# A sliding-window attention block in a fused fp32 kernel: rotary parts summed by transposes in PSUM, and the keys' cosine product on GpSimd

## What is computed

```python
def attn_layer(x, Wqkv, qs, ksc, Wo):
    q, k, v = jnp.split(x @ Wqkv, 3, -1)        # 16 heads of 64
    q, k, v = (sh(q), sh(k), sh(v))
    q = l2norm(q) * qs
    k = l2norm(k) * ksc
    freqs, scale = rotary_tables(n)
    cos, sin = (jnp.cos(freqs), jnp.sin(freqs))
    q = q * cos * scale + rotate_half(q) * sin * scale
    inv = 1.0 / scale
    k = k * cos * inv + rotate_half(k) * sin * inv
    out = local_attention(q, k, v)              # windows of 32: each sees itself and the one before
    return out.transpose(0, 2, 1, 3).reshape(b, n, INNER) @ Wo
```

## Time and profile before

| | us |
|---|---|
| median of 3 runs | 5173.48 |
| lowest and highest | 5169.82, 5185.4 |
| the profiled execution | 5172.85 |
| its span, first to last instruction | 5170.8 |

### The profile page before, as it was taken

One profiled execution on the slowest core, in us unless ns is written; L12 is line 12 of the kernel. 1 busy time (PEld: TensorE's weight loads), 2 busy tenths in 40 slices (PEclk: granted clock), 3 DMA queues, 4 the chain that ended last, 5 costly groups with the idle time before them and its releaser, 6 DMA issues. The chain is left out here.

```text
span 5170.8 us, 110439 instructions
## 1 busy us (share of the span) xinstructions
PE 3934.8 (76%) x39280; PEld 2903.7 (56%) x39280; DVE 4374.4 (85%) x7725; ACT 3040.4 (59%) x4888; POOL 2537.9 (49%) x1612
## 2 busy tenths in 40 slices
PE   5777777777777777767858678777787787777787
PEld 4655655656656646625535466466465565565565
DVE  8988989979979979954335399799799899898897
ACT  4765756746747747722413477477476476575575
POOL 5645646636636636611010266366366365464562
PEclk8988999989989989986978899899899998899899
DMA  1000000000000000021030000000000000000000
GB/s 47 8 23 11 7 22 12 8 27 6 7 27 7 8 25 8 8 62 26 2 74 1 33 7 7 26 8 21 13 8 20 14 8 19 15 7 22 12 7 12
DMA packets 30608, 88.57 MB, mean 17 GB/s; under 512 B 7505, under 2 KB 13649, under 8 KB 28369
## 3 DMA queue, kind: packets, MB, share of 16 engines
q1 hardware_dynamic: 29104, 80.95, 5.9%
q10 hardware_dynamic: 1152, 3.15, 0.2%
HBM read 38.72 MB, written 1.05 MB: 8 GB/s over the span
## 5 line engine op out<-in xcount | busy, mean ns | idle before, releaser
L771 POOL TENSOR_TENSOR pool<-pool 128x512 f32<-128x512 f32 x768 | 1069.1, 1413 | 968.3 <-DVE pool L869 968.3
L776 POOL TENSOR_TENSOR pool<-pool 128x1024 f32<-128x1024 f32 x384 | 1072.8, 2794 | 168.0 <-DVE pool L880 147.2
L443 PE MATMUL psum<-squares,pool 128*128 128x128 f32 x3072 | 475.4, 304 | 420.8 <-POOL pool L776 259.9
L443 PEld LDWEIGHTS psum<-squares,pool 128*128 128x128 f32 x3072 | 368.9, 153 | 587.2 <-issue 338.1
L880 DVE TENSOR_TENSOR pool<-pool 128x1024 f32<-128x1024 f32 x384 | 678.6, 1806 | 6.8
L483 PE MATMUL psum<-wqkv_hi,xs_lo 128*128 128x512 f32 x1152 | 522.2, 453 | 200.3 <-DVE pool L849 104.6
L646 ACT COPY pool<-psum 64x512 f32<-64x512 f32 x768 | 447.1, 582 | 367.1 <-PE psum L443 361.7
L474 PE MATMUL psum<-pool 128*64 128x128 f32 x6144 | 560.7, 296 | 116.7 <-ACT pool L661 116.5
L420 PE MATMUL psum<-pool 128*128 128x128 f32 x3072 | 455.4, 309 | 130.2 <-ACT pool L646 129.8
L859 DVE TENSOR_REDUCE pool<-pool 128x16 f32<-128x1024 f32 x384 | 449.9, 1210 | 88.1 <-ACT pool L685 88.0
L420 PEld LDWEIGHTS psum<-pool 128*128 128x128 f32 x3072 | 420.4, 219 | 179.4 <-ACT pool L646 167.8
(11 more groups left out here) (165 smaller groups left out, 8247.6 us busy)
## 6 DMA issues: line engine op xcount, KB each, us to landing
pool<-pool SPq DMA_DIRECT2D x192, 128.0 KB, 2.3
pool<-in_wqkv SPq DMA_DIRECT2D x12, 1536.0 KB, 6.0
k_st<-turn_st SPq DMA_DIRECT2D x8, 1536.0 KB, 21.3
pool<-in_wo SPq DMA_DIRECT2D x12, 512.0 KB, 3.6
pool<-in_w SPq DMA_DIRECT2D x12, 341.0 KB, 3.0
pool<-in_w SPq DMA_DIRECT2D x12, 192.0 KB, 2.9
rotary<-in_rotary SPq DMA_DIRECT2D x2, 1024.0 KB, 5.4
pool<-in_scale SPq DMA_DIRECT2D x12, 128.0 KB, 6.2
```

What stands on the lines that cost most here:

```text
L443: last = pe.transpose(bank(7 - p % 2)[:, P * j:P * j + P], rot[:, p // 2, 2 * c:2 * c + 2, :], ident)
L771: last = g.tensor_tensor(rot[:, q, :, hd * r:hd * r + hd], qn[:, q, :, hd * (1 - r):hd * (2 - r)], tab, ALU.mult)
L776: g.tensor_tensor(rot[:, q], rot[:, q], by_cos[:, q], ALU.add).then_inc(rot_ready, 1)
```

## The change

Three things, in the local layers alone.
1. The tensor `rot` becomes `by_sin`: the sine products stay apart from the cosine products, and the add on GpSimd is gone, with `rot_ready`.
2. Each square of 128x128 is written by two transposing matmuls with the identity: one of `by_cos` that starts the accumulation and one of `by_sin` that adds onto it in PSUM. So 32 instructions stand where 16 did, and TensorE waits for the sine products and the cosine products instead of the sum.
3. The keys' cosine product moves from VectorE to GpSimd, behind its four sine products, with a semaphore of its own (`k_cos_ready`). `cos_ready` is now raised once per unit. VectorE's one cosine product waits for the second group of query transposes of the unit before, where it waited for the keys' sum. The waits of the tables, of SyncE's load and of `qn` on `cos_ready` are split into two.

```diff
@@ tables
-                eng.wait_ge(cos_ready, done(layer * UNITS - 1, 2, 1))
+                eng.wait_ge(cos_ready, done(layer * UNITS - 1))
+                eng.wait_ge(k_cos_ready, done(layer * UNITS - 1))
@@ sync, before load_projections
                         sp.wait_ge(sin_ready, done(last, 2, 1))
-                        sp.wait_ge(cos_ready, done(last, 2, 1))
+                        plain(sp)
+                        sp.wait_ge(cos_ready, done(last))
+                        sp.wait_ge(k_cos_ready, done(last))
@@ tensor, turned_scores
-                            pe.wait_ge(rot_ready, done(U, 2, 0))
+                            pe.wait_ge(sin_ready, done(U, 2, 0))
+                            pe.wait_ge(cos_ready, done(U))
...
-                                    pe.wait_ge(rot_ready, done(U, 2, 1))
+                                    pe.wait_ge(sin_ready, done(U, 2, 1))
+                                    pe.wait_ge(k_cos_ready, done(U))
...
-                                    last = pe.transpose(bank(7 - p % 2)[:, P * j:P * j + P],
-                                                        rot[:, p // 2, 2 * c:2 * c + 2, :], ident)
+                                    o = bank(7 - p % 2)[:, P * j:P * j + P]
+                                    pe.matmul(o, by_cos[:, p // 2, 2 * c:2 * c + 2, :], ident,
+                                              start=True, stop=False, is_transpose=True)
+                                    last = pe.matmul(o, by_sin[:, p // 2, 2 * c:2 * c + 2, :], ident,
+                                                     start=False, stop=True, is_transpose=True)
@@ gpsimd, step
-                                        last = g.tensor_tensor(rot[:, q, :, hd * r:hd * r + hd],
+                                        last = g.tensor_tensor(by_sin[:, q, :, hd * r:hd * r + hd],
                                                                qn[:, q, :, hd * (1 - r):hd * (2 - r)], tab, ALU.mult)
                                     last.then_inc(sin_ready, 1)
-                                    g.wait_ge(sin_ready, done(U, 2, q))
-                                    g.wait_ge(cos_ready, done(U, 2, q))
-                                    g.tensor_tensor(rot[:, q], rot[:, q], by_cos[:, q], ALU.add).then_inc(rot_ready, 1)
+                                tab = turn[:, bass.ds(t, 1), 1, :].broadcast_to([P, HEADS, DH])
+                                g.tensor_tensor(by_cos[:, 1], qn[:, 1], tab, ALU.mult).then_inc(k_cos_ready, 1)
@@ vector, step
                                 v.wait_ge(sin_ready, done(U - 1, 2, 1))
-                                v.wait_ge(cos_ready, done(U - 1, 2, 1))
+                                v.wait_ge(k_cos_ready, done(U - 1))
+                                v.wait_ge(cos_ready, done(U - 1))
...
-                                v.wait_ge(rot_ready, done(U - 1, 2, 1))
-                                for q in range(2):
-                                    tab = turn[:, bass.ds(t, 1), q, :].broadcast_to([P, HEADS, DH])
-                                    v.tensor_tensor(by_cos[:, q], qn[:, q], tab, ALU.mult).then_inc(cos_ready, 1)
+                                v.wait_ge(t_ready, done(U - 1, 4, 1))
+                                tab = turn[:, bass.ds(t, 1), 0, :].broadcast_to([P, HEADS, DH])
+                                v.tensor_tensor(by_cos[:, 0], qn[:, 0], tab, ALU.mult).then_inc(cos_ready, 1)
```

More of the change, by code:

```diff
@@ L61, in macaron_program @@
         sq_ready, qn_ready, cos_ready = sem("sq_ready"), sem("qn_ready"), sem("cos_ready")
-        sin_ready, rot_ready, turn_ready = sem("sin_ready"), sem("rot_ready"), sem("turn_ready")
+        k_cos_ready = sem("k_cos_ready")
+        sin_ready, turn_ready = sem("sin_ready"), sem("turn_ready")
         t_ready, t_out, v_out = sem("t_ready"), sem("t_out"), sem("v_out")
@@ L98, in macaron_program @@
                        xc_ready, diag_ready, xn_ready, hid_ready, x_ready, var_step, aff_step],
-            "gpsimd": [lo_ready, w_hi, w_split, sin_ready, rot_ready, turn_ready, k_kept],
+            "gpsimd": [lo_ready, w_hi, w_split, sin_ready, k_cos_ready, turn_ready, k_kept],
         }
@@ L270, in window_half @@
             by_cos = cut(2, HEADS, DH)
-            rot = cut(2, HEADS, DH)
+            by_sin = cut(2, HEADS, DH)
             ss = cut(2 * HEADS)
```

## The result

The changed kernel takes 4698.61 us (median of 4 runs, 4692.60 to 4706.53), where the kernel before takes 5177.23 (median of 4, 5169.82 to 5185.40). The ratio is 0.9076, with a 95% interval of 0.9055 to 0.9097. The forecast was 4731. The profiled execution has a span of 4693.8 us.

What follows compares the result with a forecast made beforehand. VectorE was taken to bound the kernel at 18.27 us per unit. Per layer, first step 2.4, fourteen steps 29.4 and end 5 make 36.8; twelve layers save 442 of 5172.85, giving 4731 us, range 4630 to 4890.

Steps and rivals of the forecast that it cites:

- L146's wait of 1.59: VectorE's tiny instruction (L145 before the change) waits 1.59 us per unit for GpSimd's add; forecast to go with that add.
- The ring of 16.1 us: Chain of ScalarE and TensorE work from unit to unit, hidden by VectorE before; forecast to set the unit at 16.1 us.
- eight parts: Ring's terms: probability copies 5.18, squares 1.94, exponents 1.35, values' copy 0.62, query transposes 1.78, V products 0.79, key transposes 1.13, copies 3.28.
- the third rival: On TensorE, transposes that add cost 0.225 us each, the ring grows to 18.9 and the time is 5250; chance 0.05.
- GpSimd's product 2.4: The keys' cosine product, moved to GpSimd, takes 2.4 us there, bounds 2.38 and 2.58.
- The new wait of 1.5 us at L144's successor: VectorE, reaching L144 at 922.7, waits 1.5 us per unit for GpSimd's keys' cosine product, which ends at 924.2.
- VectorE's round 15.8: VectorE's own time per unit after the change: 18.27 - 2.37 - 1.59 + 1.5 = 15.8 us, below the ring.
- the race: VectorE's cosine product went ahead of GpSimd's second sine product by a hair at 916.78; falling behind costs 1.2 us more.
- The first rival: VectorE stays the bound: its cosine product falls behind GpSimd's second sine product, round 17.0 us, time 4883; chance 0.15.
- The second rival: TensorE's clock keeps dropping to half speed in one unit of three, 17.2 us per unit, time 4916; chance 0.08.
- The ends: Layer ends, where GpSimd's three long weight instructions catch VectorE: forecast gain 5 us per layer, bounds 1 and 9.
- The first steps: Each layer's first step, with nothing behind it, loses VectorE's second cosine product (L880): 2.4 us.

## Why the prediction was right

- **VectorE bounds the kernel before, partly by waiting for GpSimd.** Right. L146's wait of 1.59 is gone. The run with the keys' product moved alone shows the same waits growing when GpSimd gets more.
- **The ring of 16.1 us is next and sets the unit.** Right, with each of its eight parts within 0.06 us; 16.01 in sum. ScalarE waits for transposes alone, 12 transposes more in the ring add 1.33 (8 add 0.89), and 0.6 us more on VectorE add nothing in the middle of a layer.
- **A transpose that adds costs 0.11.** Right; the third rival (0.225 each) falls by the rows.
- **GpSimd's product 2.4.** Measured 2.39.
- **The new wait of 1.5 us at L144's successor, VectorE's round 15.8.** The place was wrong, and the size a third too large. L145 doesn't wait. The wait, 1.03 us, is at the cosine product, which lost the race for which the forecast gave it a hair's lead: L888 takes over 2 us in 135 of 192 units (mean 2003 ns). The round is about 15.4 in the changed kernel (16.01 less 0.6 idle), 15.6 where nothing idles. The error didn't reach the time, because either round is shorter than the ring.
- **The first rival (VectorE stays the bound at 17.0).** Its mechanism, the lost race, came about, its price didn't. It put 1.2 us on top of a round that already held the 1.5 of the other wait. But the two are alternatives: VectorE pays for the same overlap with GpSimd once, at L888 or at L145. The run with two copies less, in which VectorE doesn't idle, shows it pay either way at the same mean, 15.6. In the run with `residual` moved it pays at neither, as its 1.2 us of idle time leave GpSimd the room.
- **The clock doesn't drop.** Right: the slices of the local layers stand at 9 on the page (the lower ones lie in the global attention and at its end), the four units above have 1.00, and the span has 0.953 against 0.913. The second rival falls, and the run with the transposes doubled shows that they alone are enough for it.
- **The sum.** 442 us forecast, 477 measured between the spans. Three terms were off. All fourteen steps were taken at 16.1, but the second and third of a layer take 14.6 and 15.4, before the pipeline is full: 2.2 us a layer, 26 of the 31 by which the steps gave more (384 for 353). The ends gave 69 rather than 60 (6.1 each, but only 2 before the global attention). The first steps gave 2.0 rather than 2.4, 4 less in all.

At the ends, GpSimd's three long instructions for the next layer's weights hold up VectorE less. GpSimd and VectorE of the changed kernel, then VectorE of the kernel before:

```profile
958.95 3.37 DVE L904 TENSOR_SCALAR pool<-squares,pool 128x128 f32<-128x128 f32 x4
959.45 2.78 POOL L305 CAST wqkv_hi<-pool 128x3072 fp32r<-128x3072 f32 x1 [7.49 <-DMA pool<-in_scale]
...
962.41 5.62 POOL L310 TENSOR_TENSOR wqkv_lo<-pool,wqkv_hi 128x3072 fp32r<-128x3072 f32 x1 [0.18 <-POOL wqkv_hi L305]
...
965.96 2.36 DVE L911 TENSOR_SCALAR pool<-pool 128x512 f32<-128x512 f32 x1
968.00 4.71 POOL L317 TENSOR_TENSOR pool<-rotary,pool 128x2048 f32<-128x2048 f32 x1
969.83 4.16 DVE L823 TENSOR_TENSOR pool<-pool 128x256 f32<-128x256 f32 x4
```

```profile
1077.88 2.75 DVE L154 SCALAR_TENSOR_TENSOR pool<-pool 128x4 f32<-128x4 f32 x1
...
1080.87 5.58 DVE L153 TENSOR_TENSOR pool<-pool 128x4 f32<-128x4 f32 x1
```

With the 4.43 of the earlier trace rows the kernel before spent 12.8 us in three tiny instructions, 12.3 of it waiting. In the changed kernel the four L904, L911 and the four L823 wait about 7.0 in all: alone they take 0.87, 0.55 and 1.43. VectorE is now past that chain when the first long one starts, so it meets them with instructions that have partly run or come later. That it is a matter of how the two engines meet is read from the rows; no run tests it. It also stays open why the first steps take 9.5 us before the global attention and 11.1 behind it, and the ends 95.5 and 98.0.

## What to carry to other kernels

Add up the ring of waits that the present bound hides before you take load off that bound: it gives the new time, here within 1%. Where two engines exclude each other, count their excluding work against the stretch in which it has to fit, and charge the overlap once, not at each place where it may show. Moving work onto the other engine pays only if something leaves it in the same change; alone it cost 4.5% here.

## What was not expected of the hardware

- TensorE stood still for 3.5 us on average (84.1 us in 24 waits) at each jump back of a loop, and its instruction queue carried 431 packets instead of 209, once a unit had 8 transposes more than the changed kernel. So the changed kernel's loop has room for less than 8 transposes more per unit. The four steps of a layer in which the stops lie are 10.0 us longer than four ordinary ones, 120 us in all. The layers' ends are 5.5 us longer too, and how much of that comes from the loop isn't shown.
- Sixteen fp32 transposes more per unit raised the granted clock from 0.94 to 1.00 in the middle of a layer, with the length of a unit unchanged.
- Instructions over 128x32 elements took 1.8 to 2.0 us beside GpSimd's long ones, where they take 0.17 or 0.18 alone.
